# Heads of 16 in a chain of attentions: runs of three tile pairs on three banks each, two value steps in a gap, and two banks to one maximum or exponent

## The reference

```python
# stage names of the kernel, in order; b = 8 sequences, 512 queries, 512 keys
x += proj(attend(heads(ln(x) @ wq), heads(ln(x) @ wk), heads(ln(x) @ wv), causal=True))   # SELF0
x += proj(attend(heads(ln(x) @ wq), heads(ctx @ wk), heads(ctx @ wv)))                    # CROSS0
x += mlp(ln(x))                                                                           # MLP0
x += proj(attend(...ctx...))                     # CROSS1, weights rounded to three values
x += proj(attend(..., mask added to the scores)) # SELF2
x += proj(attend(...ctx...)); x += mlp(ln(x))    # CROSS2, MLP2
x  = attend(16 heads of 64, causal) @ wo + x     # SELF3

attend: softmax(q @ k.T * scale, axis=-1) @ v
```

## Time and profile before

| | |
|---|---|
| median of 3 runs | 4270.73 us (4268.64 to 4275.31) |
| the profiled execution | 4268.74 us; span 4267.0 us, mean granted clock 0.944 |
| PE busy | 3949.2 us, 93% of the span |
| DVE, ACT, POOL busy | 2756.7, 2414.2, 1660.3 us |

### The profile page before, as it was taken

How to read it: one execution, slowest core, us unless ns; L and a number is a source line. 1 busy time by engine, 2 the same in 40 slices (tenths; PEclk the granted TensorE clock), 3 DMA queues, 4 the chain that set the end, 5 groups by cost and what they waited for, 6 DMA issues and landing times. The chain is left out here.

```text
span 4267.0 us, 64410 instructions
## 1 busy us (share of the span) xinstructions
PE 3949.2 (93%) x20562; PEld 1985.0 (47%) x20562; DVE 2756.7 (65%) x6815; ACT 2414.2 (57%) x5093; POOL 1660.3 (39%) x1661
## 2 busy tenths in 40 slices
PE   6988999999796999999999999997988999999998
PEld 3333343333485343333333333432874555555555
DVE  3555568777365777789999978873653444444443
ACT  2444446767431566778888767774324554554553
POOL 2323322111232022137777722211326665666664
PEclk7888889999797899999999999997999999999999
DMA  4434335544001445444444355541000000000000
GB/s 94 85 61 70 62 65 105 82 82 69 24 1 26 103 79 83 76 72 85 61 62 61 57 98 86 81 77 46 1 25 6 6 11 12 11 1 12 11 6 10
DMA packets 135498, 220.30 MB, mean 52 GB/s; under 512 B 42736, under 2 KB 45168, under 8 KB 133488
## 3 DMA queue, kind: packets, MB, share of 16 engines
q1 hardware_dynamic: 135152, 216.02, 28.5%
HBM read 59.69 MB, written 5.51 MB: 15 GB/s over the span
## 5 line engine op out<-in xcount | busy, mean ns | idle before, releaser
L998 ACT ACTIVATE Pr<-ST 128x512 f32<-128x512 f32 (+3 forms) x2220 | 1157.1, 560 | 787.8 <-PE ST L547 774.0
L547 PE MATMUL ST<-stk 50*128 50x512 f32 (+3 forms) x2560 | 1006.6, 456 | 104.5 <-ACT Pr L998 75.8
L1211 DVE TENSOR_REDUCE mx<-MX 128x1 f32<-128x512 f32 x1056 | 701.3, 682 | 259.2 <-PE MX L547 257.1
L547 PE MATMUL MX<-stk 48*128 48x512 f32 (+3 forms) x1760 | 735.1, 455 | 27.6 <-issue 13.6
L1607 POOL TENSOR_SCALAR Pr<-Pr,mx 128x128 f32<-128x128 f32 (+3 forms) x512 | 549.6, 1086 | 388.9 <-DVE mx L1375 388.9
L547 PE MATMUL OV<-Pr,V 128*32 128x512 f32 (+3 forms) x4784 | 633.7, 603 | 2.9 <-ACT Pr L998 1.5
L547 PEld LDWEIGHTS MX<-stk 48*128 48x128 f32 x1760 | 313.5, 192 | 563.6 <-DVE mx L1211 257.1
L547 PEld LDWEIGHTS ST<-stk 50*128 50x128 f32 x2560 | 422.4, 191 | 286.7 <-ACT Pr L998 214.0
L1486 POOL CAST mhl<-mx 128x16 fp32r<-128x16 f32 x160 | 32.1, 201 | 899.2 <-DVE mx L1211 860.6
L1211 DVE TENSOR_REDUCE mx<-OV 128x1 f32<-128x512 f32 x480 | 327.4, 682 | 59.3 <-PE OV L547 58.3
L547 PE MATMUL OV<-stk 48*128 48x512 f32 (+3 forms) x800 | 355.3, 444 | 0.1
(11 more groups left out here) (154 smaller groups left out, 7464.9 us busy)
## 6 DMA issues: line engine op xcount, KB each, us to landing
stk<-hi SPq DMA_DIRECT2D x640, 128.0 KB, 4.8
stk<-lo SPq DMA_DIRECT2D x320, 128.0 KB, 5.4
misc<-misc SPq DMA_DIRECT2D x160, 128.0 KB
sums<-spread SPq DMA_DIRECT2D x80, 256.0 KB
misc<-in_ctx_t SPq DMA_DIRECT2D x24, 512.0 KB, 6.9
W_even<-in_w SPq DMA_DIRECT2D x4, 1024.0 KB, 5.2
W_even<-in_w SPq DMA_DIRECT2D x2, 2048.0 KB, 9.7
XH<-in_ctx_rows SPq DMA_DIRECT2D x8, 512.0 KB, 3.8
```

Of the source, the lines that this page charges most:

```text
L547: return nc.tensor.matmul(o, l, r, start=start, stop=stop)
L998: nc.scalar.activation(pr_buffer(s, u, i)[:, h, q0:S], ST[h % 2][:, q0:S], ACT.Copy if addmask else ACT.Exp).then_inc(ex_done, 2 if addmas ...
L1211: nc.vector.tensor_reduce(m, bank[:, :], AX.X, ALU.max).then_inc(mx_red, 1)
```

## The change

Only `attention(s)` and the memory plan change; MLP and SELF3 keep their order and get their banks under new names.

- Banks: max tiles and score tiles have a ring of three banks each, `MX` and `ST`, each ring one tensor over neighbouring banks. One bank, `L`, takes all the jobs that `LA` and `LB` took, in one order for which `L_NO` numbers them, with one pair of semaphores (`l_full`, `l_free`).
- The exponents of 16 tiles are kept (`prob`) where two blocks of four (three in SELF2) were.
- Order: a unit is eleven runs of three pairs (the last of two), `RUNS`. After run r stand at most: two value steps (`VALUES`, `TAIL`), and one or two whole jobs. In a stage without an added mask these are, in half 0, after run 0 the last two value steps of the unit before and one transpose, 1 the transposed maxima, 2 keys, 3 value steps, 4 queries, 5 nothing, 6 value steps, 7 maxima, 8 value steps, 9 and 10 output. In half 1 values stand after 7 and 9, maxima with the value steps after 8, and one transpose after 10.
- Evacuation: of a run of three tiles DVE and ACT take the first alone and the other two with one instruction of twice the width. DVE does so only in the cross stages; ACT not in SELF2, and in SELF0 not where the two tiles differ in width.

```diff
+RING = 3
+TILES = 8 * G
+RUNS = [range(k, min(k + RING, TILES)) for k in range(0, TILES, RING)]
+VALUES = {False: {3: (0, 1), 6: (2, 3), 8: (4, 5)}, True: {4: (0, 1), 7: (2, 3), 10: (4, 5)}}
+TAIL = {False: {0: (6, 7)}, True: {1: (6, 7)}}
+K_AT, Q_AT = {False: 2, True: 3}, {False: 4, True: 5}
...
-        MX = [pb("MX0"), pb("MX1")]
-        ST = [pb("ST0"), pb("ST1")]
-        OV = [pb("OV0"), pb("OV1")]
-        LA = pb("LA")
-        LB = pb("LB")
-        MAXB = [MX[0], MX[1], OV[1]]
+        MXT = es.enter_context(nc.psum_tensor("MX", [P, RING, 512], F32))
+        STT = es.enter_context(nc.psum_tensor("ST", [P, RING, 512], F32))
+        OUT, L = pb("OUT"), pb("L")
...
+        def before(k):
+            return k - RING if k >= RING else TILES - 2 + k if k < 2 else TILES - 3
+        def groups(r, one):
+            run = list(RUNS[r])
+            if one(run[-2]):
+                return [run[:-2], run[-2:]] if len(run) == RING else [run]
+            return [[k] for k in run]
...
+                    for r, run in enumerate(RUNS):
+                        for k in run:
+                            if on["m"]:
+                                max_tile(ATTN[m_of(s, u)][1], U + 1, 1 - half, k)
+                            if on["b"]:
+                                score_tile(U, half, k)
+                        if on["tail"] and r in TAIL[ATTN[tail_s][2]]:
+                            for i in TAIL[ATTN[tail_s][2]][r]:
+                                values(tail_s, U - 1, 1 - half, par if half else 1 - par, i)
+                        if on["b"] and r in VALUES[lag]:
+                            for i in VALUES[lag][r]:
+                                values(s, U, half, par, i)
...
+                def begin(u, name):
+                    wait(pe, l_free, L_NO[s, u, name])
...
+                def exp_tiles(u, U, tiles):
+                    k, n_k = tiles[0], len(tiles)
+                    at, i, q0 = TILES * U + k, tiles[-1] // G, P * (k // G % 4) if causal else 0
+                    wait(act, pv_done, 8 * U + i - 3)
+                    act.wait_ge(st_full, at + n_k)
+                    nc.scalar.activation(prob[:, k % 16:k % 16 + n_k, q0:S], STT[:, k % RING:k % RING + n_k, q0:S],
+                                         ACT.Copy if addmask else ACT.Exp).then_inc(ex_done, 2 if addmask else n_k)
...
-                        nc.vector.tensor_reduce(m, bank[:, :], AX.X, ALU.max).then_inc(mx_red, 1)
+                        nc.vector.tensor_reduce(m, MXT[:, k % RING:k % RING + n_k, :], AX.X, ALU.max).then_inc(mx_red, n_k)
...
+                            if on["a"] and r - 1 in (K_AT[addmask], Q_AT[addmask]) and tiles[0] == RUNS[r][0]:
+                                low_part(sa, U, half, int(r - 1 == Q_AT[addmask]))
```

More of the change, by code:

```diff
@@ L694, in values, with score_tile @@
-                def values(s, u, U, half, vpar, i):
-                    _, causal, addmask = ATTN[s]
-                    g, kt = i // 4, i % 4
+                    mm(MXB[k % RING][:, 0:k_n], q, stk[lo_p:lo_p + 3 * HD, 8 + i, 0:k_n]).then_inc(mx_full, 1)
+                def score_tile(U, half, k):
+                    _, causal, _ = ATTN[s]
+                    head, kt, k0 = k // G // 4 * 4 + k % G, k // G % 4, before(k)
+                    sb_, ub = unit(U if k >= RING else U - 1) if U > 0 or k >= RING else (s, 0)
+                    if ATTN[sb_][2] and k0 % G in BY_VECTOR:
+                        pe.wait_ge(st_masked, masked(ub, k0 // G, k0 % G) + 1)
+                    else:
+                        wait(pe, ex_done, TILES * (U if k >= RING else U - 1) + k0 + 1)
+                    lo_p, q0 = 64 * half, P * kt if causal else 0
+                    keys = stk[lo_p:lo_p + ROWS, 8 + head, P * kt:P * kt + P]
+                    mm(STB[k % RING][:, q0:S], keys, stk[lo_p:lo_p + ROWS, head, q0:S]).then_inc(st_full, 1)
@@ L698, in values @@
+                def values(s, U, half, vpar, i):
+                    _, causal, addmask = ATTN[s]
+                    g, kt, u = i // 4, i % 4, U - UNITS * ATTN_NO[s]
                     if kt == 0:
@@ L983, in high_part, with normalized @@
+                def normalized(sa, u, c):
+                    job = L_NO[s, u, ("T0", "T1")[c]]
+                    act.wait_ge(l_full, job + 1)
+                    nc.scalar.activation(hT[:, c, :], L[:, :], ACT.Identity, **scale_shift(sa, c)).then_inc(l_free, 1)
+                def high_part(sa, u, U, half, kind):
+                    act.wait_ge(l_full, L_NO[s, u, "KQ"[kind]] + 1)
                     for g in range(2):
@@ L985, in high_part @@
                     at = (C_K, C_Q)[kind] + 2 * ATTN_NO[sa] + half
[L986 removed]
+                    nc.scalar.activation(hi[:, kind, :], L[:, :], ACT.Identity, bias=cols[:, at:at + 1]).then_inc(hi_done, 1)
                 def product_out(U, g):
@@ L1199, in max_tile, with output_sum, max_tiles @@
+                def output_sum(end, job, part):
+                    dve.wait_ge(l_full, job + 1)
+                    add_to_x(end[1], part, Lt, l_free)
+                def max_tiles(sm, U, half, tiles):
                     _, causal, addmask = ATTN[sm]
-                    at = 32 * U + 4 * i + qt
-                    waits(dve, (mx_full, at + 1), apart=addmask or causal)
-                    bank, m = MAXB[(4 * i + qt) % 3], mx[:, half, i // 4, qt, i % 4:i % 4 + 1]
+                    k, n_k = tiles[0], len(tiles)
+                    qt = k % NT
+                    waits(dve, (mx_full, TILES * U + k + n_k), apart=addmask or causal)
+                    bank, m = MXB[k % RING], mx[:, half, k:k + n_k]
```

445 lines of the change are left out of this document (208 added, 237 removed).

## The result

The changed kernel takes 4522 us (median of 4 runs, 4506 to 4527) against 4273 us for the kernel before on the same chip: ratio 1.057, 95% interval 1.054 to 1.061. The forecast was 4210 us, faster. The time lies well outside its range.

A forecast was written before the change was run, and what follows sets the result against it. PE's work and waits were taken to set the end, with DVE bounding SELF2. From 4268.7 us: cross stages +2, clock +32, SELF0 -90, SELF2 -5 gave 4208, so 4210 as median; range 4105 to 4312 with rivals.

The forecast's parts named there:

- PE's work and the pair reads: Cross stages: PE's work falls from 56.3 to 52.2 us a batch; pair reads take 1.22 us on DVE, 1.03 on ACT.
- second pair of run 6: Cross units: it gets its bank 3.2 us behind run 5's first pair, a wait of 2.0 us in each unit.
- DMAs are the same in number and length; SP's order is the same: Transfers: nothing added for them; half 1's maxima rows are issued some 4 us ahead of the unit needing them, which hides them.
- DVE's instructions are the same in number and width ... I take -5: SELF2: DVE bounds it nearly alone; its idle time allows at most -37 us, longer gaps up to +24; taken as -5.
- the bound of +24 us for the longer gaps: SELF2: gaps after runs 7 and 10 of 3.8 us outlast the 3.1 us three banks hold for DVE: up to +3 a batch.
- 59.9 and +32 us for the clock: Cross stages: a batch takes 59.9 us, against 59.8 before; the clock falls in one unit of four, 12 x 2.7 = +32 us.
- where I had 34: The three cross stages together: +2 us for their 24 batches and +32 us for the clock.
- SELF0: -90 us: SELF0: a batch takes 57.5 us, 11.2 less than 68.7, so -90 us over 8 batches.
- the clock falls in each unit: Rival, cross stages: a clock fall in all 48 units, +130 us, gives 4308 us, slower than before; chance 0.20.
- the time behind run 5: Cross units: 3.8 us behind run 5's start holds only 1.6 us of PE's work, so the clock may fall.
- The two-bank reads, which I took as neutral: Cross stages: two single reads would free the second bank 0.6 us earlier; the batch stays at 59.9 against 59.8 us.

The follow-up runs named there:

- e2: The changed kernel with only the reciprocal (`invert`) moved, from after run 2's maxima (masked stages: run 3's) to after run 4's: 4411 us, ratio 1.031.
- e1: The changed kernel with only the LayerNorm statistics put back after runs 0 and 1 and `combine` after run 1: 4462 us, ratio 1.043.
- e4: The kernel before with only the statistics spread out (after tiles 1, 3, 5, 7) and `combine` moved from tile 4 to tile 8: 4302 us, ratio 1.0072.
- e6: e3 with each SELF2 value step in a gap of its own, and the reciprocal there one run later: 4316 us, ratio 1.009.
- e3: The changed kernel with both moves: statistics after runs 0 and 1, `combine` after run 1, reciprocal after run 4: 4340 us, ratio 1.015.
- e7: e3 with value steps 2 and 3 apart in stages without added masks, step 2 after run 5, step 3 after run 6: 4287 us, ratio 1.0033.
- e9: e3 with the edits of e6 and e7 together, still with two banks per read: 4262 us, ratio 0.995.
- e11: e9 with all maxima and exponents read one bank at a time: 4205 us, ratio 0.983.
- e8: e3 with all maxima and exponents read one bank at a time: 4323 us, ratio 1.011.

## Why the prediction was wrong

- **PE's work and the pair reads: right.** Run 0.89 for 0.90, two steps 1.86 for 1.85, reads 1.22 and 1.02 for 1.22 and 1.03, second pair of run 6 3.07 for 3.2, half 0 unit 30.07 for half a batch of 30.0.
- **"DMAs are the same in number and length; SP's order is the same": the first step that failed.** The sentence is true and was the wrong question. I costed when transfers are issued, and not who waits for them at a new place: `invert` moved ahead on DVE past the landing of `few`. I never listed it as a part of the change. Moved back behind the landing, it gives 111 us (e2), waits and the clock behind them.
- **SELF2, "DVE's instructions are the same in number and width ... I take -5": the second.** The number was the same and the place was not. `combine`, with the statistics ahead of it, went from tile 4 to tile 11 while POOL's `rows_scale` kept its place ahead of mask adds. That cost 60 us in the new order (e1; 45 of them in SELF0, 11 in SELF2) and, for four tiles, 30 us in the old one (e4). Moreover, the bound of +24 us for the longer gaps was far too low: with both placements mended SELF2 is still 104 us over before (681 against 578). Of this, two steps in one gap make 24 us by the medians and 41 by the profiled executions (e6 against e3). What part the lower clock has (0.84 for 0.95) and what makes the rest is open. My bound counted DVE's reserve of banks at full clock only.
- **The cross stages: the steady batch was right once the reciprocal is out of the way, the stage was not.** 59.9 and +32 us for the clock over 24 batches make 61.2; e3 has 61.3 in the steady parts. But the three stages together take 64 us more than before where I had 34: the first two batches of a stage are longer, 67.9 and 71.8 us in CROSS1 (57.6 and 61.9 before), and the clock falls 23 times where I had 12. Why the starts are slow no run tests. e7 shows that the named place, runs 5 and 6, was what cost: with a value step between them the three stages take 1373 us (1376 before).
- **SELF0: -90 us; e3 has -84, the changed kernel -20.** The term was right for the order of the tiles; the same two placements took the rest (in e1 SELF0 is at 567, in e2 at 596).
- **The rival "the clock falls in each unit"** was closer than its chance of 0.20 said. It decided from 36 falls in 48 units on; the granted clock of the changed kernel falls 37 times in the cross stages (twice before), though in 28 of the 46 units that the table's windows hold and not in each, and stands at 0.95, 0.94 and 0.94 in the three. Its cause, the time behind run 5, was one of two: the falls go from 37 to 27 without DVE's wait for the transfer (e2), and from 23 (e3) to 6 without the two runs in a row (e7). In the windows of e9 and e11 the clock is 1.00 through the same ring of banks.
- **The sum.** The forecast is 312 us short. 182 of it are the two placements. The other 130 are 150 in the profiled executions (18 us of the difference are e3's profiled execution over its median, 2 what the forecast added for that): SELF2's term 109, the cross stages 30 (64 where I had 34), MLP0 9, SELF0 6, the rest -4. The two-bank reads, which I took as neutral, cost 1.6 us a cross batch once runs 5 and 6 no longer stand together, and MLP0's 9 us seem to go with them: that column, which has units of a cross stage at both ends, is 341 to 347 us in the kernels with DVE's pair reads and 335 to 339 in those without.

## What to carry to other kernels

When a hand-written order is rewritten, list every instruction that waits on another engine or on a DMA, and compare its place with the landing or with the waiter's place in the other queue, and not only the number and the order within a queue. Two jobs on DVE of some 0.35 us each, moved by three and seven tiles (the second with the statistics ahead of it), cost 182 us here. A bank that several jobs share is emptied at once, even if the engine that empties it must wait for it, and a wide read that saves an engine time can cost the engine that waits for the second bank. The kernel that came out (e11: runs of three, single reads, `combine` early, `invert` late, in the stages without an added mask a value step between runs 5 and 6, in SELF2 one value step to a gap) takes 4205 us, 1.7% less than the kernel before.

## What the runs showed that I had not expected

- SELF2's steady batch is 85.3 us in the changed kernel, in e1, e2, e3, e7 and e8, though their waits there differ (POOL's longest for `combine` is 9.5 us in one and 4.0 in another). No row of waits names what sets this pace, but the granted clock repeats with it. In e3 it falls five times a batch, each time 85.3 us after the same fall of the batch before. Windows just before and just behind one of the five, in three batches (columns as in the earlier trace rows):

```profile
2123.80:2126.80 3.00, 2.68 (x15) 1.12 (x11) 2.86 (x8) 2.95 (x7) 1.70 (x2) 1.00 0.13 46
2127.30:2130.30 3.00, 3.00 (x4) 1.28 (x5) 2.32 (x7) 2.12 (x5) 2.54 (x2) 0.50 0.01 5
2209.10:2212.10 3.00, 2.69 (x15) 1.12 (x11) 2.87 (x8) 2.96 (x6) 1.71 (x2) 1.00 0.13 46
2212.60:2215.60 3.00, 3.00 (x4) 1.24 (x5) 2.31 (x7) 2.14 (x5) 2.54 (x2) 0.50 0.01 5
2294.50:2297.50 3.00, 2.69 (x15) 1.06 (x11) 2.94 (x8) 2.95 (x7) 1.65 (x2) 1.00 0.15 49
2298.00:2301.00 3.00, 3.00 (x4) 1.17 (x4) 2.25 (x7) 2.08 (x5) 2.54 (x2) 0.50 0.01 5
```

Batch and clock seem to hold each other in step; which of them leads no run shows.

- Up to 336 extra matmuls in SELF2 cost nothing that can be measured; PE's clock rises with them (0.87 to 0.94).
- Moving the reciprocal shortens the steady cross batch by 3.0 us (64.8 to 61.8), about its own wait of 3.1; over the three cross stages it is 83 us, since their first batches gain more. The fall of the clock behind the wait is visible all the same: in the unit shown, after PE had worked 1.28 of 3 us, the next product ran at 1.2 GHz, in 3.78 us instead of 1.98.
